# Second attention of a four-stage transformer kernel: two banks for the sums with outputs written over them, two ring banks, peaks carried into the last chunk, steps ordered anew

## The reference

```python
q = (x @ Wq.T).reshape(B, T, H, Dh)
k = (x @ Wk.T).reshape(B, T, H, Dh)
v = (x @ Wv.T).reshape(B, T, H, Dh)
q = _apply_rope(q, cos, sin)
k = _apply_rope(k, cos, sin)
scores = jnp.einsum('bthd,bshd->bhts', q, k) * scale
scores = jnp.where(causal[None, None], scores, -jnp.inf)
attn = jax.nn.softmax(scores, axis=-1)
y = jnp.einsum('bhts,bshd->bthd', attn, v).reshape(B, T, H * Dh)
return y / 3.0 @ Wo.T
```

## Time and profile before

| | us |
|---|---|
| median of 3 runs | 1872.32 (1872.08 to 1874.7) |
| the profiled execution | 1881.76 |
| its span | 1879.9 |
| PE busy | 1692.9 (90%) |
| PE weight loads busy | 1455.0 (77%) |
| DVE busy | 1385.8 (74%) |
| ACT busy | 1246.8 (66%) |
| POOL busy | 1080.7 (57%) |

### The profile page before, as it was taken

The page is one execution under the profiler, slowest core; times in us unless marked ns, Lnnn a source line. Parts: engine busy times, 40 slices in busy tenths (PEclk is TensorE's granted clock), DMA queues, the critical chain, the costliest instruction groups (busy, mean ns, idle before and its releaser), DMA issues.

```text
span 1879.9 us, 37204 instructions
## 1 busy us (share of the span) xinstructions
PE 1692.9 (90%) x11566; PEld 1455.0 (77%) x11566; DVE 1385.8 (74%) x3739; ACT 1246.8 (66%) x3255; POOL 1080.7 (57%) x1098
## 2 busy tenths in 40 slices
PE   6898988999689799899889979989988998998899
PEld 4677966778578688778778868877877887887688
DVE  7368863665778697787878879788796887888453
ACT  4336633354386777778678787887867877787642
POOL 2533106453266667666676676766667667666742
PEclk9999999999799999999999999999999999999999
DMA  8742067440166767577595776858759576576800
GB/s 295 217 76 42 24 195 227 87 91 1 35 113 96 137 105 138 102 130 138 80 160 106 124 122 108 145 104 134 134 84 160 96 133 106 102 137 109 154 16 31
DMA packets 636132, 215.95 MB, mean 115 GB/s; under 512 B 587296, under 2 KB 622752, under 8 KB 635808
## 3 DMA queue, kind: packets, MB, share of 16 engines
q1 hardware_dynamic: 625568, 200.71, 54.8%
q0 software_dynamic: 10368, 12.85, 4.1%
HBM read 51.06 MB, written 19.80 MB: 38 GB/s over the span
## 4 chain that ended last, share of the span: by engine, by line
PE 42%; DVE 19%; ACT 13%; issue 8%; POOL 8%; DMA 8%; another core or an unknown queue 1%; SPq 1%; ACTq 0%; POOLq 0%; DVEq 0%
PE phase_scores L1277 8%; DMA phase_pt<-phase_split 7%; ACT phase_p L1311 5%; POOL phase_split L2314 5%; PE phase_ring L166 4%; PE phase_y L166 3%; PE phase_ring L168 3%; PE phase_ring L167 3%; PE phase_y L167 3%; PE phase_y L168 3%; DVE phase_peaks L1290 3%; PE phase_banks L777 2%; DVE phase_ring L2601 2%; ACT phase_split L2298 2%; DVE phase_crossed L2599 2%
## 5 line engine op out<-in xcount | busy, mean ns | idle before, releaser
L2314 POOL TENSOR_TENSOR phase_split<-phase_p,phase_split 128x512 f16<-128x512 f32 (+3 forms) x640 | 650.2, 1016 | 272.8 <-ACT phase_split L2298 233.5
L1311 ACT ACTIVATE phase_p<-phase_scores,phase_bias 128x512 f32<-128x512 f32 (+3 forms) x680 | 418.3, 626 | 101.7 <-DVE phase_bias L2309 76.2
L2298 ACT ACTIVATE phase_split<-phase_p 128x512 f16<-128x512 f32 (+3 forms) x640 | 340.4, 577 | 62.9 <-DMA phase_pt<-phase_split 62.3
L166 PE MATMUL phase_y<-phase_pt,phase_v_hi 128*128 128x256 f16 (+1 forms) x1152 | 312.8, 272 | 21.3 <-DVE phase_y_lo L2638 20.3
L1290 DVE TENSOR_REDUCE phase_peaks<-phase_scores 128x1 f32<-128x512 f32 (+1 forms) x408 | 265.7, 667 | 67.4 <-PE phase_scores L1277 64.3
L167 PE MATMUL phase_y<-phase_pt,phase_v_hi 128*128 128x256 f16 (+1 forms) x1152 | 309.7, 269 | 0.0
L1277 PE MATMUL phase_scores<-phase_k_hi,phase_q_hi 128*128 128x512 f32 (+3 forms) x640 | 255.0, 398 | 54.8 <-ACT phase_p L1311 42.7
L168 PE MATMUL phase_y<-phase_pt,phase_v_lo 128*128 128x256 f16 (+1 forms) x1152 | 304.1, 269 | 0.0
L1277 PE MATMUL phase_scores<-phase_k_hi,phase_q_lo 128*128 128x512 f32 (+3 forms) x640 | 236.0, 369 | 0.0
L1277 PE MATMUL phase_scores<-phase_k_lo,phase_q_hi 128*128 128x512 f32 (+3 forms) x640 | 235.2, 368 | 0.0
L2677 POOL TENSOR_TENSOR sb_x<-sb_x,phase_part 128x512 f32<-128x512 f32 x128 | 164.5, 1285 | 120.7 <-ACT phase_part L2535 114.5
(11 more groups left out here) (306 smaller groups left out, 4473.3 us busy)
## 6 DMA issues: line engine op xcount, KB each, us to landing
phase_pt<-phase_split SPq DMA_TRANSPOSE x640
y_rows<-phase_zero SPq DMA_DIRECT2D x16, 512.0 KB, 7.5
phase_e_up<-expert_up SPq DMA_DIRECT2D x16, 352.0 KB
phase_e_dn<-expert_down SPq DMA_DIRECT2D x16, 256.0 KB
xn_rows<-phase_ln_xn SPq DMA_DIRECT2D x8, 512.0 KB, 2.9
sb_x<-y_rows POOLq DMA_DIRECT2D x8, 512.0 KB, 6.5
late_raw_qk<-qk SPq DMA_DIRECT2D x16, 256.0 KB, 3.3
phase_logits_t<-expert_up SPq DMA_DIRECT2D x8, 352.0 KB
```

Source lines behind the costliest of these rows:

```text
L166: pe.matmul(out, left_hi[c], r_hi, start=first and c == 0, stop=False)
L1311: act.activation(self.p_room(act, key)[:, 0:width], self.scores[:, at:at + width], ACT.Exp, bias=self.bias[:, t % 2:t % 2 + 1], accum_out= ...
L2298: act.activation(hi, value, ACT.Copy).then_inc(*self.t_hi.one)
L2314: pool.tensor_tensor(lo, value, hi, ALU.subtract).then_inc(*self.t_lo.one)
```

## The change

Four things, all in the second attention.

1. The ring has two banks instead of three, and `y` has two instead of one, taken by turns (`y_bank`). `out` no longer takes a ring bank: it writes over the sum that it was made from, in the same `y` bank. The first block of a pair therefore waits for `parted` of the pair two before. `y_hi`, `y_lo` and `part` are doubled, so `round` and `out` on ACT wait for the pair two before. The two flips of the late norm chunk use the `y` banks.
2. The last chunk's fused operation starts from the peak of the chunks before, and writes the tile's peak itself. For tiles 0 to 7 the closing reduce is gone; for tiles 8 to 15 it stands ahead of the wait for the last chunk. The bias then comes from one operation, as before.
3. All five tables are new, and so are the leads: `s` starts 21 blocks late instead of 42, and most other leads are nearer to zero.
4. At the end of the stage, some norm steps of the next stage have anchors that stand behind the last exp or turn.

The diff, cut to its core:

```diff
-    SCORE_BANKS, RING_BANKS = 4, 3
+    SCORE_BANKS, RING_BANKS, Y_BANKS = 4, 3, 1
...
-    "pe": ("SssSsspsssssSSspsssosssSSSSspsssssssssSSSpsSsosssssssSSSssssSsssvSSoSpSSssSvvssSSoSpssvSSSossssssvoSSSSssssssssv"
+    "pe": ("SSpSsssSpssssssssssssSSSSpsssssSSSsvSooSpSSsSsvssoSSSpssssSsSSsvvoSsSSpssSSsssSssssvvoSSSSsssssssssSSSSsvvoSSSSp"
...
-    "pe": {"S": 0, "s": -42, "p": 2, "o": -3, "v": 0, "b": 1},
-    "act": {"x": -2, "T": -5, "f": 1, "o": -4, "y": -3, "v": 0, "l": 0, "q": 1, "w": 1},
+    "pe": {"S": 0, "s": -21, "p": 2, "v": 0, "o": -2, "b": 1},
+    "act": {"x": 0, "T": -1, "f": 1, "y": -2, "v": 0, "o": -2, "l": 0, "q": 1, "w": 1},
...
-    BANKS = ("ring", "scores", "y")
+    BANKS = ("ring", "y", "scores")
-    RING = ("project", "values", "bound", "out", "flip", "next_flip")
+    RING = ("project", "values", "bound", "next_flip")
+    RING_BANKS, Y_BANKS = 2, 2
...
+    def dve_peak_of_chunk(self, dve, key):
+        h, t, c = key
+        if c < t // 4:
+            super().dve_peak_of_chunk(dve, key)
+            return
+        at, w, before = self.bank(key) * BANK, self.width(t, c), NEG
+        scores, top = self.scores[:, at:at + w], self.top[:, t % 2:t % 2 + 1]
+        if c:
+            dve.wait_ge(*self.peaked[h, t, c - 1])
+            before = self.peaks[:, t % 2, 0:1]
+        if c > 1:
+            before = self.peaks[:, t % 2, 3:4]
+            dve.tensor_reduce(before, self.peaks[:, t % 2, 0:c], AX.X, ALU.max).then_inc(*self.topped.one)
+            dve.wait_ge(*self.topped[h, t])
+        dve.wait_ge(*self.scored[key])
+        dve.tensor_tensor_reduce(scores, scores, self.core.hide[:, CH - w:], 1.0, before, ALU.add, ALU.max, top).then_inc(*self.peaked.one)
...
-        dve.tensor_reduce(top, self.peaks[:, t % 2, 0:t // 4 + 1], AX.X, ALU.max, negate=True).then_inc(*self.topped.one)
-        dve.wait_ge(*self.topped[key])
...
-        dve.tensor_scalar(bias, top, self.SHARE, None, ALU.add).then_inc(*self.biased.one)
+        dve.tensor_scalar(self.bias[:, t % 2:t % 2 + 1], self.top[:, t % 2:t % 2 + 1], -1.0, self.SHARE, ALU.mult, ALU.add).then_inc(*self.biased.one)
...
+    def y_bank(self, key):
+        return self.y[:, (key[0] * G + key[1]) % 2 * BANK:][:, 0:BANK]
...
-                if j == 0 and (old := self.before((h, g))):
-                    pe.wait_ge(*self.y_lo_done[old])
+                if j == 0 and (old := self.before((h, g), 2)):
+                    pe.wait_ge(*self.parted[old])
+                elif j == 0:
+                    pe.wait_ge(*self.norm.lo[self.tag, NCH - 1, g])
...
-                bank = self.ring_bank(step)
+                bank = self.y_bank(key)
                 pe.wait_ge(*self.y_lo_done[key])
                 pe.wait_ge(*self.w_lo["wo"][h,])
-                self.pe_ring_wait(pe, step)
```

More of the change, by code:

```diff
@@ L2250, in with_norms @@
         if engine in ("pe", "act", "dve"):
-            after((score, 0, 2, 0), ("flip", late, 0), ("flip", late, 1))
+            flips = [("flip", late, 0), ("flip", late, 1)]
+            if engine == "act" and order.index(("finish", 0, 2)) < order.index(("exp", 0, 2, 0)):
+                at = order.index(("finish", 0, 2))
+                order[at:at] = flips
+            else:
+                after((score, 0, 2, 0), *flips)
         for c in AHEAD:
@@ L2267, in ring_read @@
     def ring_read(self, step):
[L2268 to L2271 removed]
+        if step[0] == "next_flip":
+            return self.next.lo[(self.next.tag, *step[1:])]
+        return {"bound": self.bound_kept, "project": self.qk_done, "values": self.v_lo_done}[step[0]][step[1:]]
     def p_room(self, act, key):
@@ L2529, in act @@
                 act.wait_ge(*self.wrought[key])
-                if old := self.before(key):
+                if old := self.before(key, 2):
                     act.wait_ge(*self.added[old])
@@ L2676, in pool @@
                 pool.wait_ge(*self.parted[key])
-                pool.tensor_tensor(rows, rows, self.part[:], ALU.add).then_inc(*self.added.one)
+                pool.tensor_tensor(rows, rows, self.part[:, g % 2], ALU.add).then_inc(*self.added.one)
                 idle = self.added[key]
```

62 lines of the change are left out of this document (30 added, 32 removed), and 6 rows, old and new, of the table LEAD.

## The result

The changed kernel takes **1787.0 us** (median; 1785.4 to 1790.0), beside 1872.2 us for the kernel before in the same comparison: ratio 0.954, 95% interval 0.952 to 0.956. It is 85 us faster. The forecast of 1843 us had the sign and about a third of the size, and its range, 1812 to 1874, did not reach this far down.

A forecast was written before the change was run, and what follows sets the result against it. The stage was taken as bound by PE plus its waits, loops through ACT and DVE. Against 1881.8 us: -41 (`y_lo`) -5 (peak) +6 (transposes) +11 (given back) = -29, 1852.8; median 9.4 lower: 1843 us, range 1812 to 1874.

The forecast's parts named there:

- The waits for `y_lo`: PE's waits for `y_lo` fall from 58.7 to 17 us through two banks for the sums: gain 41 us.
- R: Hand-over from a pair's last block through ACT and DVE to `out`: 1.6 us, fitted to the trace's 58.7 us of waits.
- The freed rooms: The new order frees pair rooms earlier, SP's 275.8 and ACT's 62.3 us waits all but go; nothing counted on PE.
- Given back: Waits taken away return at PE's next loop, the score banks: 11 us lost, waits for exps at 40 to 60 us.
- The quarter: The share of the 41 us gain assumed to return as other PE waits: 11 us.
- Transposes late: In the new order transposes may land after the pair's first block needs them, narrowest at tile 15: cost 6 us.
- Rival C: Slower: transposes late at tiles 15, 11 and 13; 1895 us if score to landing takes 18 us; chance 0.13.
- Small waits: PE's waits for the bounds and the ring's 4.1 us at the stage's start: no gain or cost added.
- The clock: PE's stretches at a lower clock, named among the other 3 us or so lost a head; no term given.
- The peak: Carried peak: about 0.19 us off the path from score to bias, 5 us of PE's waits gained, at most 11.
- Rival A: DVE is the bound, so only its 20 us less work counts: 1852 us; chance 0.16.
- Rival B: All 41 us come back as waits for exps at the score banks: about 1870 us; chance 0.11.

The follow-up runs named there:

- e1: The changed kernel with the old order (tables and leads of the kernel before): 1942.2 us, ratio 1.032 to the kernel before.
- e6: The changed kernel with two pair rooms for the transposed blocks instead of three: 1855.0 us, ratio 0.986 to the kernel before.
- e2: The changed kernel with the old order and the old peak search, leaving mainly the banks and rooms for `y`, `out` and `part`: ratio 1.032 to the kernel before.
- e9: The changed kernel with the old order, two `values` and the `bound` moved later to avoid ring conflicts: 1903.6 us, ratio 1.018 to the kernel before.
- e10: As e9, with a fourth pair room and only one room for `part`: 1881.3 us, ratio 1.004 to the kernel before.
- e4: The kernel before with four pair rooms for the transposed blocks instead of three: 1856.1 us, ratio 0.987.
- e8: The changed kernel with three outs of a period one or two steps later on TensorE: ratio 0.963 to the kernel before.
- e11: The changed kernel with two outs of a period later on TensorE: ratio 0.963 to the kernel before.
- e12: The changed kernel with one out a period, the last of an even head, later on TensorE: 1817.2 us, ratio 0.971 to the kernel before.
- e3: The kernel before with the carried peak alone: 1884.7 us, ratio 1.001.
- e7: The changed kernel without the carried peak, the tile's peaks reduced at its end as before: 1792.5 us, ratio 0.954 to the kernel before.
- e15: As e14, with the load of the next head's output weights behind the exps and that head's first out one score later: 1811.9 us, ratio 0.964.
- e13: The kernel before with two `part` steps a period later in ScalarE's and GpSimd's orders alone: 1880.7 us, ratio 1.000.
- e14: As e12, with ScalarE's exps of the next tile ahead of that out's `part`, GpSimd's add behind that tile: 1819.9 us, ratio 0.967 to the kernel before.

## Why the prediction was wrong, and where it was right

**The waits for `y_lo`, right in size, and in part by luck.** The distances in the new table said 17 us, the trace has 19.3; none stands in front of a first block, and none for `parted`, which was put at nothing. R, the 1.6 us that the prediction took for the hand-over, also fits e1 (48 us expected, 47.2 measured). But e6 has the same distances on PE and 48.5 us: the term holds only where no long wait stands ahead of `y_hi` in ScalarE's list, and the prediction never made that a condition. It was also written as the gain of the banks. By e1, e2, e9 and e10 it is the gain of banks and order together, and the banks in the old order cost time.

**The freed rooms, "I count nothing for it on PE": the step that failed by the most.** The prediction had both sides in hand: ScalarE's 62.3 us at the rooms and a hand-over that runs through ScalarE. It forecast that the waits would go (SyncE 12.6 us, ScalarE 3.3, both within what it named) and priced that at 0. e4 prices it at 25 us in the old order and e6 at 60 in the new, with the mechanism in e6's rows: a hand-over of 1.6 us is one that happens when ScalarE is free, and the wait at rooms keeps it from being so. e6 also says how much of this the sum lacked. Its profiled execution is 65.5 us longer than the changed kernel's: 29.2 in waits for `y_lo`, 5.6 in waits for exps, 8.1 in other idle time, and 22.6 in PE's busy time, at a mean clock of 0.978 as before. The 29.2 the sum had, under the name of the banks. The other 36 are part of the 63 us between -29 and -92 that it missed.

**Given back, +11 us: wrong in sign here.** Waits for exps were to be 40 to 60 us; they are 25.7, 17 us fewer. The mechanism exists (e8, e11, e12, where more is given back than won, in e12 since the wait stood inside a longer one). Why it did not strike in the change is argued and not shown: there ScalarE's and VectorE's lists moved along with TensorE's. What the runs show is that one room more in the old order takes waits for exps to 31.6 us (e4), and that with the rooms short again in the new order they are 31.3 (e6). The quarter was the one term without a row, as the prediction itself said.

**Transposes late, +6 us, of which 2.0 us came.** Rival C needed a path of 17 us from score to landing. With one wait of 2.0 us for a transpose in the trace no path was that long, the prediction's own argument against C.

**Small waits, left out.** The 8.5 us before the bounds and 4.1 us at the ring are gone. They are 12.6 us that the table of steps could have shown.

**The clock, left out.** The first paragraph named "stretches at a lower clock" among PE's losses, and no term followed. 19.1 us of busy time went, with the same instructions; by e6 they hang on the rooms, since there the busy time is 1696.4 us again.

**The peak, -5 us: nothing.** e3 and e7 say 0 within 0.4%. VectorE does not even work less: 1385.8 us busy before, 1391.2 in e3. Of the small reduces saved, 128 x 0.157 = 20 us, 13 are eaten by a start value read from SBUF in 192 operations; why the busy time is not 7 us less but 5 more is open. The prediction bounded that by 0.06 us an operation and took 0; the rows of e3 say 0.062 to 0.079, the upper bound and a little more:

```profile
L2316 DVE CUSTOM_DVE_ANT_0 phase_scores<-phase_scores,sb_hide,phase_peaks 128x512 f32<-128x512 f32 x48 | 36.4, 759 | 2.5 <-PE phase_scores L1277 0.9
...
L2316 DVE CUSTOM_DVE_ANT_0 phase_scores<-phase_scores,sb_hide 128x512 f32<-128x512 f32 x16 | 10.9, 684 | 0.0
```

**Rival A, VectorE as the bound, is refuted as a bound.** The kernel passed the 1852 us that it gave, with as much work on VectorE. The sign that the prediction had set for it, VectorE above 84% busy, came all the same: 1040 us of work are over 84% of any stage shorter than 1238 us, so it could not tell A from a large gain. A returns in a smaller form: in single stretches, as in e15's rows, VectorE is what all wait for. The Trainium skill ("Perfetto Trace Analysis", section "Identifying the Most-Contended Engine") names the engine with the highest occupancy as the one to improve, with TensorE judged by its weight loads. In this stage that was VectorE before (1045 us against 1021) and after (1040 against 1006), and 85 us were had with 5 us less work on it. **Rival B's** own sum, -41 + 41 - 5 + 6, gives 1873 us and not about 1870, which changes nothing here.

**Summed up:** forecast -29, measured -92 between the two profiled executions. `y_lo` -39 for -41; exps -17, where the peak and the given back were +6; bounds and ring -13 for 0; transposes +2 for +6; other idle time about -6; busy time at the better clock -19 for 0. In terms of waits the second, third and last are what was missed. In terms of causes, by e6, 36 of the 63 us missed hang on the free rooms in the new order; the other 27 come with the rest of the change and were not divided further.

**What stays open.** The 94 us between e10 and the changed kernel were not divided further: the two tables differ nearly everywhere, and no mixed ones were run. The second room for `part` and the anchors of the norm steps were not tried alone. e6 shows that the new order without the early rooms loses 60 us, which a room added to the old one does not win (25 us in e4, 22 to 25 from e9 to e10). So rooms and order do not add up. The rows of e6 show where half of its loss arises, one hand-over a period; why the old order has no such place as costly was not looked into. No version tried beats the changed kernel.

## What to carry to other kernels

A hand-over between engines has no duration of its own: it is as long as what stands ahead of it in each in-order list, so before a gain is worked out from one, look for the long waits in those same lists and price what happens to the hand-over when they go. The sum of a wait does not say what it is worth: ScalarE's 50.2 us at `part` moved on to other steps and gave nothing (e13), 28 us off its 62.3 at the rooms gave 25 (e4), and PE's longest repeated wait for `y_lo` stood inside a longer one for an exp (e12). Before a wait is booked as a gain, ask what the engine would wait for next, and until when. A second buffer is a permission that the order has to use, and buffer and order are one change, to be measured and forecast as one.

## What the runs showed of the hardware

**Waits of TensorE are followed by a lower clock.** Five stretches of the kernel before and two of the changed one (columns as in the earlier trace rows, the clock before the last two):

```profile
804.00:808.00 4.00, 3.94 (x30) 3.06 (x28) 3.61 (x7) 2.00 (x5) 3.16 (x5) 1.00 0.96 174
808.00:812.00 4.00, 1.66 (x12) 1.54 (x13) 2.96 (x9) 4.00 (x13) 3.34 (x3) 0.91 0.81 150
812.00:816.00 4.00, 4.00 (x25) 3.41 (x24) 3.75 (x14) 3.08 (x11) 1.24 (x3) 0.66 1.17 130
...
1436.00:1440.00 4.00, 1.29 (x13) 1.08 (x11) 2.60 (x8) 3.41 (x10) 2.90 (x3) 0.92 0.91 148
1440.00:1444.00 4.00, 3.94 (x19) 3.55 (x19) 3.83 (x9) 3.07 (x11) 2.76 (x3) 0.50 0.95 170
```
```profile
884.00:888.00 4.00, 2.90 (x22) 2.13 (x20) 3.82 (x11) 2.90 (x9) 2.91 (x4) 1.00 0.00 2
888.00:892.00 4.00, 3.30 (x14) 2.33 (x13) 3.21 (x12) 3.85 (x11) 2.38 (x4) 0.66 0.09 20
```

After PE had been busy for 1.29 of 4 us its granted clock stood at 0.50 for the next four, the lower of its two levels, 1.2 GHz; in the stretches at 0.66 it was there for part of the time. PE looks fully busy in them and starts 19 or 25 matmuls (of mixed shapes) where 804 to 808 us at full clock has 30. Over the 17 kernels here the mean clock follows PE's idle time roughly. Estimated as span times missing share, in one profiled execution each, e1 with 233 us idle lost 58 us by it (1940.5 x 0.030), the kernel before 41 at 187, e6 41 at 157, the changed kernel 20 at 114. From the changed kernel to the one before that is 22 us of clock for 73 of idle time, to e1 38 for 118, to e6 21 for 43: three to five tenths of a microsecond on top of each that PE waits, which was missing in every term of the prediction. It is no fixed price: e4 paid 0.25, and e12, with 18 us more idle time than the changed kernel, 26 us (1.4), e14 with 25 more only 11.

**A start value read from SBUF** lengthened the fused search for a peak on VectorE from 684 to 759 ns at 512 columns, from 547 to 626 at 384 and from 429 to 491 at 256 (e3).
